# A fused attention and feed-forward layer on one core: the rows of the maxima issued by ScalarE, a longer loop body, and a rearranged beginning

## The reference, cut to what matters

```python
q = (route @ wq + bq).reshape(b_, r_, k_, H, D)     # H = 8 heads, D = 16
k = (route @ wk + bk).reshape(b_, r_, k_, H, D)
v = (route @ wv + bv).reshape(b_, r_, k_, H, D)
scores = jnp.einsum('brkhd,brnhd->brknh', q, k) / D ** 0.5
attn = jax.nn.softmax(scores, axis=3)
out = jnp.einsum('brknh,brnhd->brkhd', attn, v).reshape(b_, r_, k_, m_)
x = _layernorm(route + out @ wo + bo, ln1_g, ln1_b)
ff = jax.nn.relu(x @ w1 + b1) @ w2 + b2             # FF = 512
return _layernorm(x + ff, ln2_g, ln2_b)
```

## Time and profile before

| | us |
|---|---|
| median of three executions | 4288.4 |
| the profiled execution, its own time | 4295.68 |
| its span, first to last instruction | 4293.6 |
| TensorE busy | 4178.0 (97%) |
| VectorE busy | 3694.2 (86%) |
| GpSimd busy | 3616.9 (84%) |
| ScalarE busy | 3424.5 (80%) |
| mean granted TensorE clock | 0.994 |

### The profile page before, as it was taken

The page is one execution under the profiler, slowest core; times in us unless marked ns, Lnnn a source line. Parts: engine busy times, 40 slices in busy tenths (PEclk is TensorE's granted clock), DMA queues, the critical chain, the costliest instruction groups (busy, mean ns, idle before and its releaser), DMA issues.

```text
span 4293.6 us, 151787 instructions
## 1 busy us (share of the span) xinstructions
PE 4178.0 (97%) x50954; PEld 3638.6 (85%) x50954; DVE 3694.2 (86%) x9739; ACT 3424.5 (80%) x5889; POOL 3616.9 (84%) x4620
## 2 busy tenths in 40 slices
PE   5999999999999999999999999999999999999998
PEld 4888888888888888888888888888888888888886
DVE  5888888888888888888888888888888888888886
ACT  3888887878888887888888877888887888888886
POOL 4888888888888888888888888888888888888887
PEclk8999999999999999999999999999999999999999
DMA  5555655555656565555555555555565556555562
GB/s 124 145 148 146 154 144 149 146 141 147 153 141 154 145 152 145 145 148 150 148 146 152 147 141 148 144 149 151 144 155 138 149 145 155 146 150 148 146 154 59
DMA packets 1294636, 621.92 MB, mean 145 GB/s; under 512 B 636544, under 2 KB 1293696, under 8 KB 1293824
## 3 DMA queue, kind: packets, MB, share of 16 engines
q1 hardware_dynamic: 1024016, 477.81, 45.7%
q10 hardware_dynamic: 269808, 133.99, 10.7%
HBM read 135.40 MB, written 67.11 MB: 47 GB/s over the span
## 4 chain that ended last, share of the span: by engine, by line
PE 77%; SPq 9%; issue 5%; DMA 3%; DVE 3%; ACT 2%; POOL 2%; ACTq 0%; DVEq 0%; POOLq 0%
PE s_ps L681 10%; PE oT_ps L708 10%; PE bankB L667 10%; PE bankC L646 9%; PE bankC L667 9%; PE sT_ps L695 9%; SPq L246 7%; PE bankB L646 7%; PE bankA L721 5%; PE bankA L771 4%; DMA stack<-parts 3%; PE bankA L646 3%; PE bankB L640 2%; SPq L240 2%; PE oT_ps L764 1%
## 5 line engine op out<-in xcount | busy, mean ns | idle before, releaser
L398 ACT ACTIVATE prob_sb<-sT_ps 128x1024 f32<-128x1024 f32 x1024 | 1044.2, 1020 | 610.9 <-PE sT_ps L695 595.1
L511 DVE TENSOR_REDUCE max_sb<-s_ps 128x8 f32<-128x1024 f32 x1024 | 1213.2, 1185 | 17.0 <-PE s_ps L681 14.6
L271 POOL TENSOR_TENSOR parts<-rest_sb,parts 128x512 bf16<-128x512 f32 x512 | 585.8, 1166 | 223.5 <-ACT parts L372 223.5
L681 PEld LDWEIGHTS s_ps<-stack 96*128 96x128 bf16 x8192 | 463.8, 98 | 307.9 <-issue 243.3
L681 PE MATMUL s_ps<-stack 96*128 96x128 bf16 x8192 | 639.6, 221 | 54.3 <-DMA stack<-parts 25.7
L695 PE MATMUL sT_ps<-stack 99*128 99x128 bf16 x8192 | 629.0, 219 | 1.3 <-ACT prob_sb L398 1.3
L708 PE MATMUL oT_ps<-prob_sb,v_ones 128*32 128x128 f32 x16384 | 553.6, 276 | 3.0 <-ACT prob_sb L398 2.2
L667 PE MATMUL bankB<-w_sb,h_sb 128*128 128x128 f32 x4096 | 525.4, 281 | 7.3 <-ACT h_sb L379 6.6
L708 PEld LDWEIGHTS oT_ps<-prob_sb,v_ones 128*32 128x32 f32 x16384 | 416.3, 109 | 128.2 <-DVE max_parts L609 69.2
L695 PEld LDWEIGHTS sT_ps<-stack 99*128 99x128 bf16 x8192 | 504.3, 98 | 3.0 <-ACT prob_sb L398 1.8
L667 PE MATMUL bankC<-w_sb,h_sb 128*128 128x128 f32 x4096 | 499.2, 275 | 0.0
(11 more groups left out here) (78 smaller groups left out, 8721.1 us busy)
## 6 DMA issues: line engine op xcount, KB each, us to landing
stack<-parts SPq DMA_DIRECT2D x3072, 128.0 KB, 2.6
x_blocks<-in_x SPq DMA_DIRECT2D x1024, 64.0 KB, 2.1
out<-out_sb ACTq DMA_DIRECT2D x256, 256.0 KB, 3.5
x_sb<-in_x ACTq DMA_DIRECT2D x255, 256.0 KB, 3.1
stack<-max_parts SPq DMA_DIRECT2D x768, 8.0 KB, 3.1
w_sb<-in_L_conv_w SPq DMA_DIRECT2D x2, 256.0 KB, 3.0
x_sb<-in_x SPq DMA_DIRECT2D x1, 256.0 KB, 3.1
be_row<-in_L_conv_ln_b SPq DMA_DIRECT2D x2, 64.0 KB, 5.3
```

The source lines that it names most:

```text
L271: pool.tensor_tensor(parts[:, r % 2, 3 * c + LO], rest_sb[:, c], parts[:, r % 2, 3 * c + MID], ALU.subtract).then_inc(lo_split, 1)
L398: act.activation(prob_sb[:, s % 2], sT_ps[:], ACT.Exp, scale=float(D) ** -0.5).then_inc(exp_done, 1)
L511: dve.reduce_max(max_sb[:, (r - lag) % 2, :, s], s_ps[:].rearrange("p (h k) -> p h k", h=H), AX.X).then_inc(max_done, 1)
L681: ins = pe.matmul(s_ps[:, h * P:(h + 1) * P], stack[0:PROD, (r - lag) % 4, 0, h, tok], stack[0:PROD, (r - lag) % 4, 1, h, tok], start=True ...
```

## The change

It does four things. The three DMAs of the rows of the maxima are issued by ScalarE, between its two `relu` calls, and not by SyncE. The loop body holds 120 steps and not 48 (it is then gone through twice and jumps back once; the steps in the loop are the same 240). The ones in the stack are written as float32 words that hold two bf16 ones, half of them by VectorE before anything else, half by GpSimd, and the second GpSimd memset after step 0 is gone; the small constants are set before `v_ones`. The 16 DMAs that load wo and bv by head are issued by ScalarE (after one small exponential), and VectorE turns the first x before it splits wq and wk.

```diff
-UNROLL = 48
+UNROLL = 120
@@ SyncE
-            for h in range(H):
-                at = (h % HU) * VW + (h // HU) * D
-                sp.dma_start(wo_sb[at:at + D], wo[h * D:(h + 1) * D]).then_inc(consts_loaded, DMA)
-                sp.dma_start(bv_col[at:at + D], col(bv[h * D:(h + 1) * D]),
-                             allow_slow_non_contiguous=True).then_inc(consts_loaded, DMA)
...
-                if live(t, r, 2):
-                    sp.wait_ge(max_parts_made, upto(t, r, 2, plus=1))
-                    for part in range(MAXROWS):
-                        sp.dma_start(stack[PROD + part:PROD + part + 1, (r - 2) % 4, 0],
-                                     max_parts[:, part]).then_inc(max_rows_loaded, DMA)
@@ GpSimd
-            pool.memset(v_ones[:], 1.0).then_inc(consts_set, 1)
             pool.memset(minus_half[:], -0.5).then_inc(consts_set, 1)
             pool.memset(minus_one[:], -1.0).then_inc(consts_set, 1)
             pool.memset(eps_sb[:], EPS).then_inc(consts_set, 1)
-            pool.wait_ge(consts_set, N_SET)
-            pool.memset(stack[PROD:PROD + MAXROWS, 0:2, 1], 1.0).then_inc(stack_ones_set, 1)
+            pool.memset(v_ones[:], 1.0).then_inc(v_ones_set, 1)
+            pool.wait_ge(v_ones_set, 1)
+            pool.memset(stack[PROD:PROD + MAXROWS, 2:4, 1].bitcast(F32), TWO_ONES).then_inc(stack_ones_set, 1)
...
             step(0, 0)
-            pool.wait_ge(lo_split, 2)
-            pool.memset(stack[PROD:PROD + MAXROWS, 2:4, 1], 1.0).then_inc(stack_ones_set, 1)
@@ ScalarE
-            act.wait_ge(qk_loaded, N_QK * DMA)
+            act.wait_ge(consts_set, N_SET)
+            act.activation(pause_act[:], minus_one[:, 0:1], ACT.Exp)
+            for h in range(H):
+                at = (h % HU) * VW + (h // HU) * D
+                act.dma_start(wo_sb[at:at + D], wo[h * D:(h + 1) * D]).then_inc(consts_loaded, DMA)
+                act.dma_start(bv_col[at:at + D], col(bv[h * D:(h + 1) * D]),
+                             allow_slow_non_contiguous=True).then_inc(consts_loaded, DMA)
...
                 if live(t, r, 5):
                     relu(t, r, 5, 0)
+                if live(t, r, 2):
+                    act.wait_ge(max_parts_made, upto(t, r, 2, plus=1))
+                    for part in range(MAXROWS):
+                        act.dma_start(stack[PROD + part:PROD + part + 1, (r - 2) % 4, 0],
+                                      max_parts[:, part]).then_inc(max_rows_loaded, DMA)
+                if live(t, r, 5):
                     relu(t, r, 5, 1)
...
+            act.wait_ge(qk_loaded, N_QK * DMA)
+            act.wait_ge(v_ones_set, 1)
             step(0, 0)
@@ VectorE
+            dve.memset(stack[PROD:PROD + MAXROWS, 0:2, 1].bitcast(F32), TWO_ONES).then_inc(stack_ones_set, 1)
+            turn_x(0, 0)
             dve.wait_ge(qk_loaded, N_QK * DMA)
```

More of the change, by code:

```diff
@@ L25 @@
+import numpy as np
 import concourse.bass as bass
@@ L50 @@
 PROD = len(Q_PARTS) * D
+TWO_ONES = float(np.array([0x3F803F80], np.uint32).view(np.float32)[0])
 STACK_DMAS = 2 * len(Q_PARTS)
 MAXROWS = 3
-UNROLL = 48
+UNROLL = 120
 LEAD = 8
@@ L84, in build @@
         minus_half, minus_one, eps_sb = (sb(n, [P, SEQS]) for n in ("minus_half", "minus_one", "eps_sb"))
-        pause = sb("pause", [P, 1])
+        pause, pause_act = sb("pause", [P, 1]), sb("pause_act", [P, 1])
         x_sb = sb("x_sb", [P, 2, SEQS, P])
@@ L117, in build @@
         ident_zero, ident_set, consts_set = sem("ident_zero"), sem("ident_set"), sem("consts_set")
-        stack_ones_set = sem("stack_ones_set")
+        stack_ones_set, v_ones_set = sem("stack_ones_set"), sem("v_ones_set")
         bv_wide_set, w_products_done, consts_made = sem("bv_wide_set"), sem("w_products_done"), sem("consts_made")
@@ L190, in iterate, with col @@
                 step(0, r)
-        N_QK, N_CONST, N_SET, N_MADE = 5, 11 + 2 * H, 4, 4
+        N_QK, N_CONST, N_SET, N_MADE = 5, 11 + 2 * H, 3, 4
         block = ctx.enter_context(nc.Block())
+        def col(v):
+            return v.rearrange("(p a) -> p a", a=1)
         @block.sync
@@ L198, in row @@
                 return v.rearrange("(a m) -> a m", a=1).broadcast_to([P, P])
-            def col(v):
-                return v.rearrange("(p a) -> p a", a=1)
             def by_feature(v):
@@ L346, in step @@
                     lo_part(t, r, 1)
-            pool.wait_ge(stack_ones_set, 1)
+            pool.wait_ge(stack_ones_set, 2)
             step(0, 0)
-            pool.wait_ge(lo_split, 2)
-            pool.memset(stack[PROD:PROD + MAXROWS, 2:4, 1], 1.0).then_inc(stack_ones_set, 1)
-            pool.wait_ge(stack_ones_set, 2)
             pool.wait_ge(consts_loaded, N_CONST * DMA)
@@ L457, in step @@
                     apply2(t, r, 6, 0)
-            act.wait_ge(consts_set, N_SET)
+            act.wait_ge(qk_loaded, N_QK * DMA)
+            act.wait_ge(v_ones_set, 1)
             step(0, 0)
@@ L466, in _, with turn_x @@
         def _(dve):
+            dve.memset(stack[PROD:PROD + MAXROWS, 0:2, 1].bitcast(F32), TWO_ONES).then_inc(stack_ones_set, 1)
+            def turn_x(t, r):
+                dve.wait_ge(blocks_loaded[r % 2], upto_dma(t, r, 0, per=P // BLK * DMA))
+                if (v := upto(t, r, 0)) is not None:
+                    dve.wait_ge(v_done, v)
+                if (v := upto(t, r, 0)) is not None:
+                    dve.wait_ge(xT_lo, v)
+                dve.transpose(xT_sb[:], x_blocks[:, r % 2]).then_inc(x_turned, 1)
+            turn_x(0, 0)
             dve.wait_ge(qk_loaded, N_QK * DMA)
@@ L562, in step @@
                 row_max(t, r, 1)
[L563 to L569, removed]
+                if live(t, r, 0) and (r > 0 or not isinstance(t, int)):
+                    turn_x(t, r)
                 if live(t, r, 6):
@@ L792, in _ @@
             pe.wait_ge(stack_ones_set, 2)
+            pe.wait_ge(v_ones_set, 1)
             iterate(pe, step, 1, LEAD, LAST, 6)
```

## The result

The changed kernel takes 4572.15 us (median of 4 runs, 4561.64 to 4574.66) beside 4288.45 us before: the ratio is 1.065, 95% interval 1.063 to 1.067. It is 284 us slower. The profiled execution has a span of 4570.1 us, 276.5 us more than before's 4293.6.

The account below looks back on a forecast made before the run. The steady 16.15 us step with TensorE 97% busy was taken to set the time. 4295.7 + 269 - 30 - 21 - 12 = 4502 us for the profiled execution, 4494 against the median; range 4400 to 4590, chance 0.65.

Parts of the forecast that it names:

- The step that decides: ScalarE between its relus: three issues of about 1.9 us delay v's copy 1.37 us; TensorE loses 1.07 us a step.
- signs that the prediction named: Changed profile: z_sb every 17.2 us, L447 ending 3.1 us or more after L609, L721 idle about 1 us, one 4 us gap.
- moved rows: Row DMAs issued on ScalarE: TensorE loses 1.07 us in each of 251 steps, +269 us.
- waits for the stack: Score matmuls waiting for stack DMAs, 37.8 us in 52 places: should go almost entirely, -30 us (15 to 38).
- hold-ups: Issues on ScalarE sometimes held up: as upper end, 2.2 us for three on average, TensorE losing up to 1.47 a step, +369.
- upper rival: Held-up issues fall on ScalarE more often because two queues issue at once: +369 us, near 4600; chance 0.08.
- Issues faster on ScalarE: Rival: row issues on ScalarE at L452's price, +93 to +143 us, time 4318 to 4368 us; chance 0.12.
- issues that lie beside the activations: Rival: second relu and v's copy already queued during the issues, TensorE loses nothing, 4225 us; chance 0.12.
- Loop body: Jumps back in the step loop: four become one, 7 us each, -21 us (bounds 0 and -21).
- Beginning: Before the steady steps: shorter memset and earlier first x start TensorE near 11.3, not 17.40; together -12 us (6 to 15).

Follow-up runs that it names:

- filler kernel: Changed kernel with the three rows issued by SyncE again and three 128x512 scratch copies on ScalarE between the two relus; 4525.82 us, ratio 1.057 to before.
- one_row: Changed kernel with ScalarE issuing one of the three row DMAs and SyncE two; 4252.12 us, ratio 0.993 to before; again 4255.20 us, 0.992.

## Why the prediction was right, and where it was off

- **That it gets slower, and by which wait: right.** The step that decides was that the three issues hold the second `relu` and with it the copy of v. The loss was to be 1.07 us in each of 251 steps, and an undisturbed step is 1.00 us longer: 1.82 us of issues put the second `relu` 1.36 us later relative to `max_parts`, and of the 0.46 us of margin 0.35 was usable (the projection started 0.11 us after the copy of v). The filler kernel shows this wait with no DMA moved. Of the signs that the prediction named, `z_sb` came every 17.15 us, L449 ended 3.13 us after `max_parts`, and at the one jump left TensorE's score weights came after an idle time of 3.5 us, not 4.
- **The size: 4494 predicted, 4572 measured, inside the range.** For the moved rows and the waits for the stack together the prediction had 269 - 30 = 239 us, and alone this part cost 312.6. The term that was mis-sized is the hold-ups. The prediction took 1.9 us for three issues, from one timeline row and a median, and counted 30 us less for the waits for the stack. Those waits did fall, by 27 us in that count and 26 us with each taken once. But the three issues take 2.04 us in the mean, as they did on SyncE (2.06), where hardly anything waited for them. That is 0.22 us beyond the median in 249 steps, 54 us. A least-squares fit of the step lengths in this trace (jump and first steps left out) gives each microsecond of these hold-ups a price of 1.0 us; to those of L454 and L457 in the step before it gives 22 us, and to the 48 us at half clock 22 us. The same fit for before finds 9 us for the held-up stores, nothing for the clock, and 22 us for the waits for the stack. These shares are estimates: a fit shows what goes together, not what causes what. The row that told of the hold-ups was there, L240's longest issue of 1.93 us and the 1.52 us of L455; it was used as an upper bound where a mean over the 768 issues could have been taken. With that mean, 2.06 and not 1.9 us, the sum would have been 40 us higher, 4534; the other issues and the clock would still have been missing.
- **The upper rival was the nearer one** (near 4600): held-up issues in the chain. Its reason holds in part at most. The three row issues' mean is no longer than on SyncE, but the issue of the load of `x_sb` went from 0.403 to 0.522 us in the mean, and 27 of its 255 took over 0.9 us where none did before. Of those 27, 93% had a code-fetch packet beside them; whether the second queue has a part in it is open.
- **Issues faster on ScalarE, and issues that lie beside the activations: both wrong.** 0.609 us at the median against SyncE's 0.591, and 1.25 us of idle time before the activation behind them. The Trainium skill's rule that other engine instructions can be queued while a control instruction executes ("Advanced Engine Details and Errata", section "Sequencer Loop") does not hold here for an activation behind the issue: it waited in every kernel whose issues outlast the activation ahead of them. What was queued before the issue does go on: in `one_row` the 0.53 us issue lies under the first `relu`.
- **Loop body: right.** -21 predicted, -18 measured alone, -23 in the account of the steps.
- **Beginning: right,** -12 predicted and measured alone (4278.67 against 4290.24), 9.5 at the first `z_sb`. TensorE's start was forecast at 11.3 and came at 11.54, the second turn of x at 22 and came at 23.42. Which of the rearrangements brought how much was not separated.
- **The price of an issue beside its transfer.** The Trainium skill's sentence that issuing from several engines saves the sequencer's time, which is "usually small relative to the DMA itself" ("DMA: Bandwidth & Descriptors", section "Issuing engines are not separate DMA queues"), is no guide to the loop: there one issue took 0.61 us of the 2.2 us that passed from its start to the landing of the data (medians), and 1.8 us for three stood in the chain, where the transfers did not (DMA 0%).

## What to carry to other kernels

An issue occupies the engine that makes it, though the profile doesn't count it as busy: add its measured time (0.40 us for L452, 0.61 us for L441) to that engine's load, and look at what stands behind it in its program before looking at its busy share. It is free only as far as it fits under the work already queued ahead of it and the slack of what comes next; here one of three did. And price it by its mean with the hold-ups, since in the chain each of them counts, while on SyncE, which only issues, nearly all were absorbed.

## What was unexpected about the hardware

- The three row issues are held up, by over 0.3 us together, in three of ten steps (76 of 256 before, 75 after), on SyncE as on ScalarE; before, a long issue took 0.6 to 1.1 us more in half of the cases, and nearly always a code-fetch packet started beside it (357 of 363).
- How long an issue takes also depends on where it stands: the second row's issue takes 0.61 us in most steps when one engine issues all three, and 0.87 us in 106 of 249 steps when SyncE issues the third.
- A kernel with nearly the same undisturbed step as the changed one (17.31 and 17.15 us) but its waits at other places had the clock at half for 242 us and not 95.
- A jump back costs some 6 to 7 us with a body of 48 steps and 5 us with one of 12. A body of 12 steps did not save code fetching: 955 packets against 776 with one of 120.
